# Attention: scores, turned maxima and turned outputs in one ring of three PSUM banks, read by VectorE alone

## The chip, the cores and the metric

The kernel runs on one core of a Trainium2 chip. The metric is the time of one execution in microseconds (us); the median of three runs is given. The engines are TensorE (PE, with its weight loads shown apart as PEld), VectorE (DVE), ScalarE (ACT), GpSimd (POOL) and SyncE (SP), which issues the DMAs.

## The reference

Two layers over x of 4 x 1024 x 128 numbers. Each layer adds an attention and a feed-forward part to x. Both attentions have 16 heads of width 8; the first is causal over 1024 keys, the second has 342 keys, of which a query sees about the first third of its own place:

```
scores = jnp.einsum('bhqd,bhkd->bhqk', q, k)
scores = jnp.where(causal[None, None], scores, -inf)      # layer 1: + mask * -1e9
attn = jax.nn.softmax(scores, axis=-1)
out = jnp.einsum('bhqk,bhkd->bhqd', attn, v)
```

Softmax subtracts each row's maximum, which is the part of it that this change touches.

## The kernel before

The program is a chain of blocks: weights, projection, the first feed-forward part, attention of layer 0, a block between the layers, attention of layer 1, and the experts. `attention` (from L809 on) is one function for both layers.

Its unit of work is a group of four heads of one batch element: 4 batch elements of 4 groups, so 16 units a layer. A unit has two halves that work on the scores in two layouts:

- **fills** (`fill`, L971 to L991 on PE; L1104 to L1111 on DVE): PE writes a block of scores, 128 queries by up to 512 keys (or four heads by 128 keys), with a mask matmul (L984) ahead of the score matmuls (L987), into a PSUM bank. DVE reduces the bank to row maxima (L1111). There are 38 fills in a unit of layer 0 and 17 in one of layer 1. When the last is read, `tail` (L1113 to L1134) splits the maxima into three bf16 parts.
- **turn_max** (L1046, in the prologue L1066): PE turns the parts into a PSUM bank; **copy_max** (L1081) takes them from there to SBUF, and SP stores them as three more rows of the query operand (L891), so that the maxima are subtracted inside the second product.
- **pairs** (L1003) compute the scores once more, transposed, with the maxima in them; ACT takes the exponential (L1089); **weigh** (L1026) multiplies by the values into the bank `a_po`. At the end of 512 queries ACT copies `a_po` to `o_raw` (L1097), **turn_out** (L1055) turns it back with four transposes, and **scale_out** divides by the row sums on DVE (L1146 and L1149).

`batch_schedule` (L725 to L795) writes one list of entries for a batch element by planned PE time, and every engine walks the same list and does its own entries. The fills run ahead of the pairs by one unit and 13 fills. A prologue list (`first`) holds the 38 or 17 fills of the first unit and 13 of the second, with no pairs among them. In layer 0 the batch list stands in a loop for three elements and once more after it; in layer 1 it is written out four times.

PSUM has eight banks: two for fills (`a_ps`), four for the pairs (`a_pst`), one for `a_po`, and one, `p_turn` (`a_pt`), which turn_max and turn_out share. Fill k waits for the reduction of fill k-2 (L977). turn_max and turn_out wait until the former contents of `a_pt` have been read, by ACT (copy_max) or by DVE (scale_out), and the scheduler keeps a copy_max or scale_out ahead of the next turn.

Of the kernel before, what the change touches and what calls it, by code (L numbers as in the profile page):

```python
# [22 lines left out]
ALU = mybir.AluOpType  # L23
# [8 lines left out]
P = 128  # L32
# [12 lines left out]
GH = 4  # L45
# [12 lines left out]
TUNING = [(13, 2800, 300, 2200, 400), (13, 2500, 300, 2200, 200)]  # L58
# [13 lines left out]
        scores_ready maxima_done split_steps maxima_turned maxima_copied maxima_stored scores_t_ready  # L72
        exp_done unseen_zeroed pv_done v_staged o_copied o_turned inverse_done o_done""",
# [602 lines left out]
class Geometry:  # L676
# [3 lines left out]
    def __init__(self, layer):  # L680
# [33 lines left out]

        self.lead, self.tail_time, self.copy_time, self.out_time, self.scale_time = TUNING[layer]

# [8 lines left out]
    def batch_schedule(self, first, last):  # L725
# [5 lines left out]
        if first:  # L731
            return ([("fill", 0, k, 0) for k in range(self.F)] + [("tail", 0, 0, 0)]
                    + [("fill", 1, k, 0) for k in range(2)] + [(what, 0, 0, 0) for what in ("turn_max", "copy_max")]
                    + [("fill", 1, k, 0) for k in range(2, self.lead)])
# [7 lines left out]
        def weigh(step, half):  # L742
# [4 lines left out]
            if half < len(halves):  # L747
                put(4 * (halves[half][1] - halves[half][0] + FIXED), "weigh", g, n, half)
                if st["last"] and half == len(halves) - 1:
                    put(0, "end", g, st["c"], 0)  # L750
                    out.append((now + self.out_time, ("turn_out", g, st["c"], 0)))
                    out.append((now + self.out_time + self.scale_time, ("scale_out", g, st["c"], 0)))
# [17 lines left out]
        for g in range(1, GROUPS if last else GROUPS + 2):  # L770
            for k in range(self.F):
# [5 lines left out]
                if k == self.F - 1:  # L777
                    out.append((at + 1, ("tail", g, 0, 0)))
                    out.append((at + self.tail_time, ("turn_max", g, 0, 0)))
                    out.append((at + self.tail_time + self.copy_time, ("copy_max", g, 0, 0)))  # L780

        ordered, reading = [], None
        for _, entry in sorted(out, key=lambda x: x[0]):
            what, rest = entry[0], entry[1:]
            if what in ("turn_max", "turn_out"):
                if reading:
                    ordered.append(reading)
                reading = ({"turn_max": "copy_max", "turn_out": "scale_out"}[what],) + rest
            if what in ("copy_max", "scale_out"):
                if entry != reading:  # L790
                    continue
                reading = None
            ordered.append(entry)
        return ordered


def counted_before(layer):
# [4 lines left out]
    layer0 = dict(scores_ready=units * geo.F, maxima_done=units * geo.F, split_steps=units * geo.split, maxima_turned=units,  # L802
                  maxima_copied=units, maxima_stored=16 * units, scores_t_ready=2 * units * geo.S,
                  exp_done=2 * units * geo.S, unseen_zeroed=2 * units * len(geo.masked), pv_done=units * geo.S,
                  v_staged=units, o_copied=ends, o_turned=ends, inverse_done=ends, o_done=ends)
# [3 lines left out]
def attention(nc, io, sb, dram, layer):  # L809
# [5 lines left out]
    with ExitStack() as ctx:  # L815
# [24 lines left out]
        block = ctx.enter_context(nc.Block())  # L840

# [34 lines left out]
        def _(sp):  # L876
            def run(b, schedule, last):
                ends = 0
                for what, g, k, part in schedule:
# [8 lines left out]
                    if what == "copy_max":  # L888
                        sp.wait_ge(s["maxima_copied"], since["maxima_copied"] + n + 1)
# [3 lines left out]
                    if what == "next_load" and not last:  # L893
                        sp.wait_ge(s["scores_t_ready"], since["scores_t_ready"] + 2 * S * (n + 1))
                        load_operands(sp, sb, dram, layer, geo.keys, b + 1, g)

# [5 lines left out]
            run(0, geo.batch_schedule(True, False), True)  # L902
# [67 lines left out]
        def _(pe):  # L970
            def fill(b, g, k):  # L971
                f, slot = geo.fills[k], g % GROUPS
                at = (b * GROUPS + g) * F + k
# [17 lines left out]
                last.then_inc(s["scores_ready"], 1)  # L991
# [41 lines left out]
            def run(b, schedule, last):  # L1033
                turned, outs = 1, 0
                for what, g, k, part in schedule:
                    n = b * GROUPS + g
                    if what == "fill":
                        fill(b, g, k)
# [4 lines left out]
                    if what == "turn_max":  # L1043
                        pe.wait_ge(s["split_steps"], since["split_steps"] + geo.split * (n + 1))
                        pe.wait_ge(s["o_done"], since["o_done"] + b * 2 * GROUPS + outs)
                        pe.transpose(p_turn[0:top_rows.shape[0], 0:P // 2].bitcast(BF16),  # L1046
                                     top_parts[:, :, :, :].rearrange("p a j q -> p (a j q)"),
                                     sb["identb"][:, :]).then_inc(s["maxima_turned"], 1)
                        turned += 1
                    if what == "turn_out":  # L1050
                        pe.wait_ge(s["o_copied"], since["o_copied"] + 2 * n + k + 1)
                        pe.wait_ge(s["maxima_copied"], since["maxima_copied"] + b * GROUPS + turned)
                        pe.wait_ge(s["o_done"], since["o_done"] + 2 * n + k)
                        for t in range(CT):
                            last_t = pe.transpose(p_turn[:, t * P:(t + 1) * P], o_raw[:, t * P:(t + 1) * P],  # L1055
                                                  sb["ident"][:, :])
# [928 lines left out]
```

## Time and profile before

| | |
|---|---|
| three runs | 1411.87, 1413.98, 1414.88 us; median 1413.98 us |
| profiled execution | 1409.36 us, span of its profile 1407.4 us |
| PE busy | 1184.2 us, 84% of the span |
| DVE busy | 1041.5 us, 74% |
| ACT busy | 740.0 us, 53% |
| POOL busy | 566.7 us, 40% |
| mean granted TensorE clock | 0.907 of 2.4 GHz |

Attention of layer 0 runs from 246.7 to 793.7 us of the span, that of layer 1 from about 911 to 1160 us. The profile's page gives the busy time of each engine and, in 40 slices, where it lies; other views list the waits of an engine, its instructions in order of time, and sums over stretches that one chooses. A busy PE row has a modelled end, so a wait of PE is looked for in its own idle rows and in the spacing of starts.

### The profile page before, as it was taken

What the parts mean: (1) busy time and instruction counts of PE and PEld (TensorE: products, weight loads), DVE (VectorE), ACT (ScalarE), POOL (GpSimd) and SP (SyncE); (2) the same over time, 40 slices, a digit from 0 to 9 for tenths busy, and PEclk for the clock granted to TensorE, in tenths of its full rate; (3) what the DMA queues carried; (4) which work ended last, traced back from release to release, by engine and by line L of the source; (5) the groups of instructions that cost most, each with busy time, mean ns of one, the idle gap of its engine ahead of it and who ended that gap; (6) DMA issues with size and microseconds to landing.
All of it is one profiled execution on the core that took longest, in us unless ns stands there. A gap on an engine that the chain in (4) does not pass through costs nothing. (4 is left out here: it accounts for less than half of the span.)

```text
span 1407.4 us, 28130 instructions
## 1 busy us (share of the span) xinstructions
PE 1184.2 (84%) x8802; PEld 650.5 (46%) x8802; DVE 1041.5 (74%) x2108; ACT 740.0 (53%) x1137; POOL 566.7 (40%) x821
## 2 busy tenths in 40 slices
PE   0555666899989998999999767589999988999994
PEld 0333555234434443444443344335445436888872
DVE  5997997888868886888785255478778736677788
ACT  0552222056656665666567533136556666777772
POOL 5555222013322331223222155326557663456563
PEclk9987898599999999999999877569999998999996
DMA  3343870001221211121100013112222105577541
GB/s 98 97 124 94 126 92 0 16 4 56 93 81 41 75 62 55 47 69 62 40 2 3 1 57 95 39 35 64 51 61 57 50 23 196 159 237 236 188 120 60
DMA packets 98604, 107.92 MB, mean 77 GB/s; under 512 B 16225, under 2 KB 76454, under 8 KB 98480
## 3 DMA queue, kind: packets, MB, share of 16 engines
q1 hardware_dynamic: 93488, 97.83, 25.5%
q0 software_dynamic: 4992, 8.48, 1.8%
q8 instruction: 73, 1.20, 0.4%
q14 instruction: 51, 0.42, 0.1%
HBM read 64.67 MB, written 42.63 MB: 76 GB/s over the span
## 5 line engine op out<-in xcount | busy, mean ns | idle before, releaser
L1089 ACT ACTIVATE a_probs<-a_pst 128x1024 f32<-128x1024 f32 (+4 forms) x544 | 431.8, 813 | 248.6 <-PE a_pst L1003 245.9
L1111 DVE TENSOR_REDUCE a_tops<-a_ps 128x1 f32<-128x512 f32 (+9 forms) x624 | 363.0, 594 | 93.8 <-PE a_ps L987 78.2
L933 POOL TENSOR_SCALAR_AFFINE_SELECT a_probs<-a_probs 128x256 f32<-128x256 f32 (+3 forms) x384 | 182.3, 481 | 461.8 <-ACT a_probs L1089 460.0
L987 PE MATMUL a_ps<-kp,qp 96*128 96x512 bf16 (+9 forms) x1280 | 329.1, 313 | 8.6 <-issue 6.7
L1003 PE MATMUL a_pst<-qp,kp 99*128 99x512 bf16 (+4 forms) x1088 | 269.1, 335 | 3.2 <-ACT a_probs L1089 2.8
L1026 PE MATMUL a_po<-a_probs,vh 128*32 128x256 f32 (+2 forms) x3584 | 268.9, 373 | 2.5 <-POOL a_probs L933 1.5
L1111 DVE TENSOR_REDUCE a_tops_lead<-a_ps 128x1 f32<-128x512 f32 x256 | 173.0, 690 | 36.3 <-PE a_ps L987 32.8
L987 PEld LDWEIGHTS a_ps<-kp,qp 96*128 96x128 bf16 x1280 | 115.4, 103 | 101.5 <-DVE a_tops_lead L1111 34.8
L984 PE MATMUL a_ps<-mask_s,identb 128*128 128x128 bf16 (+8 forms) x624 | 148.5, 239 | 15.8 <-DVE a_tops L1111 7.1
L984 PEld LDWEIGHTS a_ps<-mask_s,identb 128*128 128x128 bf16 x624 | 60.9, 98 | 167.2 <-DVE a_tops L1111 77.7
L1644 POOL DMA_INDIRECT chosen_rows<-e_slot_y,e_slot_x x92 | 92.7, 1007 | 88.6 <-DVE e_slot_y L1832 66.6
L1003 PEld LDWEIGHTS a_pst<-qp,kp 99*128 99x128 bf16 (+1 forms) x1088 | 97.2, 101 | 67.3 <-ACT a_probs L1089 21.5
L1026 PEld LDWEIGHTS a_po<-a_probs,vh 128*32 128x32 f32 (+1 forms) x3584 | 71.4, 108 | 105.7 <-issue 76.1
L1820 DVE TENSOR_TENSOR e_tails<-e_hidden,e_heads 128x512 fp32r<-128x512 f32 x124 | 91.4, 738 | 35.2 <-ACT e_heads L1754 32.9
L1747 ACT ACTIVATE e_hidden<-e_pup,e_slot_b 128x512 f32<-128x512 f32 x92 | 63.3, 688 | 27.7 <-PE e_pup L1668 25.6
L945 POOL DMA_INDIRECT slot_rows<-rows,slots x64 | 63.2, 988 | 14.2 <-issue 12.2
L1146 DVE RECIPROCAL a_inv_sum<-a_pt 128x16 f32<-128x16 f32 x64 | 16.3, 254 | 63.3 <-PE a_pt L1055 60.8
L148 POOL TENSOR_TENSOR f_hq<-f_v,f_sc 128x704 f32<-128x704 f32 x16 | 22.2, 1385 | 85.2 <-DVE f_v L143 85.2
L594 PE MATMUL f_pt<-ident,f_hq 128*128 128x128 f32 (+1 forms) x96 | 16.1, 310 | 42.9 <-POOL f_hq L148 42.9
L632 ACT ACTIVATE f_hqt<-f_pt 128x256 f32<-128x256 f32 x32 | 12.2, 383 | 66.3 <-PE f_pt L594 66.1
L1097 ACT ACTIVATE a_o_raw<-a_po 128x512 f32<-128x512 f32 x64 | 38.2, 596 | 16.3 <-PE a_po L1026 16.1
L1055 PE MATMUL a_pt<-ident,a_o_raw 128*128 128x128 f32 x256 | 39.5, 276 | 6.5 <-ACT a_o_raw L1097 6.5
(264 smaller groups left out, 1809.4 us busy)
## 6 DMA issues: line engine op xcount, KB each, us to landing
e_slot_w<-weight_parts SPq DMA_DIRECT2D x23, 1024.0 KB, 5.4
weight_parts<-a_cut SPq DMA_DIRECT2D x18, 512.0 KB, 3.9
k_parts<-o SPq DMA_DIRECT2D x48, 128.0 KB
qp<-q_parts SPq DMA_DIRECT2D x64, 96.0 KB
kp<-k_parts SPq DMA_DIRECT2D x32, 192.0 KB
slot_rows<-empty_row SPq DMA_DIRECT2D x4, 1495.0 KB, 27.0
e_slot_x<-slot_rows SPq DMA_DIRECT2D x23, 260.0 KB, 3.5
a_raw<-in_wraw SPq DMA_DIRECT2D x18, 256.0 KB, 4.3
```

The lines of the kernel that those rows point to most:

```text
L933: pool.affine_select(out=seen, in_=seen, compare_op=ALU.is_ge, fill=0.0, base=m0, pattern=[[0, 2], [1, mw]], channel_multiplier=-1 if laye ...
L945: pool.indirect_dma_start(dram["slots"], bass.IndirectOffsetOnAxis(sb["slots"][:, choice, t:t + 1], 0), sb["rows"][:, t, :], None, bounds_ ...
L984: pe.matmul(out, sb["identb"][:, :], mask_s[r][:, 0:mw].unsqueeze(1).broadcast_to([P, nh, mw]), start=True, stop=False, skip_group_check=True)
L987: last = pe.matmul(bank[:, i * room:i * room + w], sb["qp"][slot][0:KROWS, j, f["qt"] * P:(f["qt"] + 1) * P], sb["kp"][slot][0:KROWS, j // ...
L1003: last = pe.matmul(p_st[half][0:st["rows"], i, off:CHUNK], sb["kp"][slot][0:KROWS + PARTS, half, st["kt"] * P:st["kt"] * P + st["rows"]], ...
L1026: last = pe.matmul(p_o[VW * j:VW * (j + 1), c0:c1], sb["vh"][g % 2][0:st["rows"], st["kt"], j, :], probs[local % RING][0:st["rows"], j, c0 ...
L1055: last_t = pe.transpose(p_turn[:, t * P:(t + 1) * P], o_raw[:, t * P:(t + 1) * P], sb["ident"][:, :])
L1089: act.activation(probs[local % RING][0:st["rows"], 2 * part:2 * part + 2, st["off"]:CHUNK], p_st[part][0:st["rows"], :, st["off"]:CHUNK], ...
L1111: dve.tensor_reduce(out, scores, AX.X, ALU.max).then_inc(s["maxima_done"], 1)
L1644: pool.indirect_dma_start(dram["chosen"], bass.IndirectOffsetOnAxis(slot_x[r % XR][:, t, E:E + 1].bitcast(U32), 0), slot_y[r % YR][:, t, : ...
L1747: act.activation(hidden[m % RR][:, :], p_up[m % UR][:, :], ACT.Gelu, bias=biases(j)[:, k:k + 1])\
L1820: dve.tensor_tensor(tails[m % HR][:, :], hidden[m % RR][:, :], heads[m % HR][:, :].bitcast(F32), ALU.subtract)\
```

## The change

`a_pt` and the pair of `a_ps` banks become one ring of three banks. A use of the ring is a fill, a turn_max or a turn_out. Uses are counted in the order of the list; use u goes to bank u mod 3 and waits until the use three before it has been read. One semaphore counts banks filled (by PE), one banks read (by DVE). Because a batch element has 164 uses in layer 0 and 80 in layer 1, both with remainder 2, the first two uses of a batch element find their bank two uses back and the third five back. All reads are now by DVE, in the same order: the copy of the turned maxima leaves ACT (activation Copy) and becomes a DVE `tensor_copy`. `copy_max` and `scale_out` are no longer entries with times of their own; they are done at the place of their turn. The order of PE's own entries stays as it was.

```diff
-TUNING = [(13, 2800, 300, 2200, 400), (13, 2500, 300, 2200, 200)]
+TUNING = [(13, 2800, 2200), (13, 2500, 2200)]
+BANKS = 3
+BANK_USES = ("fill", "turn_max", "turn_out")
...
+    def bank(self, use, first):
+
+        return (use + (self.uses - self.first_uses if first else 0)) % BANKS
...
+    def since_bank(self, use, first):
+
+        if first:
+            return BANKS if use >= BANKS else None
+        return next(d for d in range(1, 2 * BANKS) if (use - d if use >= d else self.uses + use - d) % BANKS == use % BANKS)
...
-        p_s = [ctx.enter_context(nc.psum_tensor(f"a{layer}_ps{i}", [P, 512], F32)) for i in range(2)]
+        p_s = [ctx.enter_context(nc.psum_tensor(f"a{layer}_ps{i}", [P, 512], F32)) for i in range(BANKS)]
...
-        p_turn = ctx.enter_context(nc.psum_tensor(f"a{layer}_pt", [P, 512], F32))
...
+            def fresh_bank(b, use, first):
+
+                behind = geo.since_bank(use, first)
+                if behind:
+                    pe.wait_ge(s["banks_read"], read(b, use - behind, first))
+                return p_s[geo.bank(use, first)]
...
-                if not (isinstance(b, int) and g == 0 and k < 2):
-                    pe.wait_ge(s["maxima_done"], since["maxima_done"] + at - 1)
-                bank, w, nh = p_s[(g * F + k) % 2], f["width"], len(f["heads"])
+                bank, w, nh = fresh_bank(b, use, first), f["width"], len(f["heads"])
...
-                    if what == "turn_out":
-                        pe.wait_ge(s["o_copied"], since["o_copied"] + 2 * n + k + 1)
-                        pe.wait_ge(s["maxima_copied"], since["maxima_copied"] + b * GROUPS + turned)
-                        pe.wait_ge(s["o_done"], since["o_done"] + 2 * n + k)
...
+            def turn_out(b, n, c, use):
+
+                pe.wait_ge(s["o_copied"], since["o_copied"] + 2 * n + c + 1)
+                turned = fresh_bank(b, use, False)
...
-                    if what == "copy_max":
-                        act.wait_ge(s["maxima_turned"], since["maxima_turned"] + n + 1)
-                        act.wait_ge(s["maxima_stored"], since["maxima_stored"] + 16 * n)
-                        act.activation(top_rows[:, :], p_turn[0:top_rows.shape[0], 0:P // 2].bitcast(BF16), ACT.Copy)\
-                            .then_inc(s["maxima_copied"], 1)
...
+            def copy_max(b, n, use, first):
+
+                turned = filled_bank(b, use, first)
+                dve.wait_ge(s["maxima_stored"], since["maxima_stored"] + 16 * n)
+                dve.tensor_copy(top_rows[:, :], turned[0:top_rows.shape[0], 0:P // 2].bitcast(BF16))\
+                    .then_inc(s["banks_read"], 1)
...
+            def scale_out(b, g, c, use):
+
+                turned = filled_bank(b, use, False)[:, :].rearrange("p (t j w) -> p t j w", t=CT, w=VW)
+                dve.wait_ge(s["banks_read"], read(b, use - 1))
```

DVE's order in the prologue of layer 0, around the end of the first unit (`a0_ps0` and so on are the banks, `tops0` and `tops1` the maxima of the two units in flight). Before:

```order
L1133 TENSOR_TENSOR a0_top_parts<-a0_top_rest,a0_top_parts 128x32
L1111 TENSOR_REDUCE a0_tops1<-a0_ps0 128x4
L1111 TENSOR_REDUCE a0_tops1<-a0_ps1 128x2
L1111 TENSOR_REDUCE a0_tops1<-a0_ps0 128x2
L1111 TENSOR_REDUCE a0_tops1<-a0_ps1 128x1
L1111 TENSOR_REDUCE a0_tops1<-a0_ps0 128x1
```

The same place with the change:

```order
L1151 TENSOR_TENSOR a0_top_parts<-a0_top_rest,a0_top_parts 128x32
L1130 TENSOR_REDUCE a0_tops1<-a0_ps0 128x4
L1130 TENSOR_REDUCE a0_tops1<-a0_ps1 128x2
L1158 COPY a0_top_rows<-a0_ps2 96x128
L1130 TENSOR_REDUCE a0_tops1<-a0_ps0 128x2
L1130 TENSOR_REDUCE a0_tops1<-a0_ps1 128x1
L1130 TENSOR_REDUCE a0_tops1<-a0_ps2 128x1
```

The reductions go round three banks, and the copy of the turned maxima (L1158) stands on DVE behind two reductions of the next unit.

DVE's order in layer 1 at the seam between two batch elements, where the last turned output of one element is scaled and the fills of the next begin. Before:

```order
L1146 RECIPROCAL a1_inv_sum<-a1_pt 128x16
L1149 TENSOR_TENSOR o<-a1_pt,a1_inv_sum 128x4x32
L1111 TENSOR_REDUCE a1_tops1<-a1_ps0 128x1
L1111 TENSOR_REDUCE a1_tops1<-a1_ps1 128x1
```

With the change:

```order
L1165 RECIPROCAL a1_inv_sum<-a1_ps1 128x16
L1168 TENSOR_TENSOR o<-a1_ps1,a1_inv_sum 128x4x32
L1130 TENSOR_REDUCE a1_tops1<-a1_ps0 128x1
L1130 TENSOR_REDUCE a1_tops1<-a1_ps1 128x1
L1130 TENSOR_REDUCE a1_tops1<-a1_ps2 128x1
L1130 TENSOR_REDUCE a1_tops1<-a1_ps0 128x1
```

The order of the work is the same; the second fill now uses the bank of the turned output just ahead of it.

## Rows read from the trace of the kernel before

**Rows 1.** Page, part 2: busy tenths in 40 slices of 35.2 us, and granted clock

```profile
PE   0555666899989998999999767589999988999994
PEclk9987898599999999999999877569999998999996
```

**Rows 2.** Busy time by stretch: PE, PEld, DVE, ACT, POOL, clock, DMA share, GB/s

```profile
core 0: us, PE busy (x) PEld busy (x) DVE busy (x) ACT busy (x) POOL busy (x), PEclk, DMA share, GB/s
248.00:283.30 35.30, 30.46 (x93) 7.61 (x94) 31.82 (x56) 1.56 (x2) 0.00 (x0) 0.56 0.06 16
252.30:286.40 34.10, 30.43 (x88) 7.94 (x87) 29.37 (x50) 3.13 (x4) 0.41 (x1) 0.50 0.06 17
300.00:790.00 490.00, 476.85 (x4344) 197.39 (x4336) 373.06 (x673) 310.26 (x417) 137.67 (x296) 0.99 0.16 50
912.70:933.00 20.30, 17.08 (x93) 6.72 (x91) 17.24 (x38) 0.27 (x1) 0.00 (x0) 0.50 0.16 47
993.00:999.70 6.70, 6.48 (x41) 3.26 (x41) 3.37 (x10) 3.93 (x6) 4.22 (x6) 0.50 0.08 22
```

**Rows 3.** Waits of PE, 300 to 790 us: total, times, longest

```profile
PE a_ps L987 <- issue: 6.7, 2, 3.4
PE a_pt L1055 <- ACT a_o_raw L1097: 2.9, 3, 1.0
PE a_pst L1003 <- ACT a_probs L1089: 0.9, 4, 0.3
```

**Rows 4.** Waits of PE, 960 to 1132 us

```profile
PE a_ps L984 <- DVE a_tops L1111: 2.6, 4, 0.8
...
PE a_pt L1046 <- DVE a_top_parts L1133: 2.1, 9, 0.2
PE a_pst L1003 <- ACT a_probs L1089: 0.6, 3, 0.2
```

**Rows 5.** DVE in time, prologue of layer 0: start, length, merged count, idle before

```profile
247.36 6.83 DVE L1111 TENSOR_REDUCE a_tops<-a_ps 128x4 f32<-128x512 f32 x11 [0.96 <-PE a_ps L987]
...
258.02 2.87 DVE L1111 TENSOR_REDUCE a_tops_lead<-a_ps 128x1 f32<-128x512 f32 x4
...
265.99 1.02 DVE L1111 TENSOR_REDUCE a_tops<-a_ps 128x1 f32<-128x384 f32 x2 [0.23 <-PE a_ps L987]
...
274.60 1.28 DVE L1111 TENSOR_REDUCE a_tops<-a_ps 128x4 f32<-128x512 f32 x2
...
282.33 2.07 DVE L1111 TENSOR_REDUCE a_tops_lead<-a_ps 128x1 f32<-128x512 f32 x3
```

**Rows 6.** PE in time, the first pairs after that prologue

```profile
283.47 1.06 PE L1003 MATMUL a_pst<-qp,kp 99*128 99x512 bf16 x2
```

**Rows 7.** Two lines (min/median/max ns) and a row of the page (busy, mean ns)

```profile
L1081 ACT ACTIVATE a_top_rows<-a_pt x32: 263/263/273, 275.1 to 1137.2; 96x128 bf16<-96x128 bf16 x32
...
L1131 DVE CAST a_top_parts<-a_top_rest x32: 181/181/182, 274.3 to 1135.9; 128x32 bf16<-128x32 f32 x32
...
L1146 DVE RECIPROCAL a_inv_sum<-a_pt 128x16 f32<-128x16 f32 x64 | 16.3, 254 | 63.3 <-PE a_pt L1055 60.8
```

**Rows 8.** All engines in time, middle of layer 0

```profile
501.14 1.98 DVE L1111 TENSOR_REDUCE a_tops<-a_ps 128x4 f32<-128x512 f32 x3
...
501.55 0.22 PE L1046 MATMUL a_pt<-identb,a_top_parts 128*96 128x128 bf16 x1
```

**Rows 9.** All engines in time, seam of two batch elements in layer 1

```profile
990.16 0.66 PE L1055 MATMUL a_pt<-ident,a_o_raw 128*128 128x128 f32 x4 [0.71 <-ACT a_o_raw L1097]
...
991.14 0.29 DVE L1149 TENSOR_TENSOR o<-a_pt,a_inv_sum 128x128 f32<-128x128 f32 x1
991.35 1.88 DVE L1111 TENSOR_REDUCE a_tops<-a_ps 128x1 f32<-128x342 f32 x4
...
991.91 0.20 PE L984 MATMUL a_ps<-mask_s,identb 128*128 128x44 bf16 x1 [0.76 <-DVE a_tops L1111]
```

More of the change, by code:

```diff
@@ L732, in batch_schedule @@
             return ([("fill", 0, k, 0) for k in range(self.F)] + [("tail", 0, 0, 0)]
-                    + [("fill", 1, k, 0) for k in range(2)] + [(what, 0, 0, 0) for what in ("turn_max", "copy_max")]
+                    + [("fill", 1, k, 0) for k in range(2)] + [("turn_max", 0, 0, 0)]
                     + [("fill", 1, k, 0) for k in range(2, self.lead)])
@@ L779, in batch_schedule @@
                     out.append((at + self.tail_time, ("turn_max", g, 0, 0)))
[L780 to L794, printed above, removed]
+        return [entry for _, entry in sorted(out, key=lambda x: x[0])]
 def counted_before(layer):
@@ L840, in attention, with filled, read @@
         block = ctx.enter_context(nc.Block())
+        def filled(b, use, first=False):
+            return since["banks_filled"] + geo.uses_before(b, first) + use + 1
+        def read(b, use, first=False):
+            return since["banks_read"] + geo.uses_before(b, first) + use + 1
         def raw_load(sp, b, i):
@@ L876, in _, with run @@
         def _(sp):
-            def run(b, schedule, last):
-                ends = 0
+            def run(b, schedule, last, first=False):
+                ends = use = 0
                 for what, g, k, part in schedule:
@@ L887, in run @@
                         ends += 1
-                    if what == "copy_max":
-                        sp.wait_ge(s["maxima_copied"], since["maxima_copied"] + n + 1)
+                    if what == "turn_max":
+                        sp.wait_ge(s["banks_read"], read(b, use, first))
                         sp.dma_start(sb["qp"][g % GROUPS][KROWS:KROWS + PARTS, :, :].rearrange("r j t -> r (j t)"),
@@ L895, in run @@
                         load_operands(sp, sb, dram, layer, geo.keys, b + 1, g)
+                    use += what in BANK_USES
             if layer == 1:
@@ L990, in fill, with turn_max @@
                                      start=not f["mask"], stop=True, skip_group_check=True)
-                last.then_inc(s["scores_ready"], 1)
+                last.then_inc(s["banks_filled"], 1)
+            def turn_max(b, n, use, first=False):
+                pe.wait_ge(s["split_steps"], since["split_steps"] + geo.split * (n + 1))
+                pe.transpose(fresh_bank(b, use, first)[0:top_rows.shape[0], 0:P // 2].bitcast(BF16),
+                             top_parts[:, :, :, :].rearrange("p a j q -> p (a j q)"),
+                             sb["identb"][:, :]).then_inc(s["banks_filled"], 1)
+            def turn_out(b, n, c, use):
+                pe.wait_ge(s["o_copied"], since["o_copied"] + 2 * n + c + 1)
+                turned = fresh_bank(b, use, False)
+                for t in range(CT):
+                    last = pe.transpose(turned[:, t * P:(t + 1) * P], o_raw[:, t * P:(t + 1) * P], sb["ident"][:, :])
+                last.then_inc(s["banks_filled"], 1)
             def pair(b, g, k, half, local):
@@ L1117, in tail @@
                 top = tops[g % 2]
-                dve.wait_ge(s["maxima_done"], since["maxima_done"] + (n + 1) * F)
+                dve.wait_ge(s["banks_read"], read(b, use - 1, first))
                 if layer == 0:
@@ L1153, in _ @@
-            run(0, geo.batch_schedule(True, False), True)
+                        tail(b, g, use, first)
+                    if what == "turn_max":
+                        copy_max(b, b * GROUPS + g, use, first)
+                    if what == "turn_out":
+                        scale_out(b, g, k, use)
+                    use += what in BANK_USES
+            run(0, geo.batch_schedule(True, False), True, first=True)
             batches(dve, run)
```

94 lines of the change are left out of this document (42 added, 52 removed).

## The prediction

> **What bounds the kernel now.** I read the slices first, then busy time by stretch, then the waits of PE in each stretch, and the timeline only where a wait stood.
>
> The slices show PE at eight or nine tenths through both attentions (slices 8 to 22, and from 28 on). But in the eighth slice the granted clock is down to 5 tenths, and it is at 5 and 6 in the 26th and 27th, where the second attention begins [rows 1]. The stretches say why. In the body of layer 0 (300 to 790 us) PE is busy 476.9 of 490 us at a clock of 0.99, DVE 373 us and ACT 310 us [rows 2]: PE bounds it, and the question is how long PE waits there for what the change touches. It waits 6.7 us at two places with releaser "issue" (the loop's turn), 2.9 us for the copy of `a_po` and 0.9 us for exponentials [rows 3]. No row of PE there waits for a reduction. So in 490 us **the two banks cost PE nothing**.
>
> The two prologues are different. They hold only fills, 51 in layer 0 and 30 in layer 1 (17 and 13), and the clock stands at 0.50, that is 1.2 GHz, from 252.3 to 286.4 us and through 912.7 to 933 us [rows 2]. DVE does the longer job, and still idles: 35.30 - 31.82 = 3.5 us in the first, 20.30 - 17.24 = 3.1 us in the second [rows 2]. Each fill waits for the reduction two before it, and at the low clock it comes too late for DVE. In layer 1 there is a third place: the seam between batch elements, where PE waits 0.76 us for a reduction after 0.71 us for `a_po` [rows 9]; rows 4 give 2.6 us over the three seams.
>
> **The change part by part.** The sum is made against the profiled execution, 1409.36 us, which lies 4.6 us under the median of 1413.98; I apply the difference to the median.
>
> *Third bank, prologue of layer 0.* Two 384-wide reductions that follow without a wait take 1.02 us, so starts are 1.02 - 0.55 = 0.47 apart (one alone is 0.55); two 512-wide ones take 1.28, so 1.28 - 0.69 = 0.60 apart; but four 512-wide ones in the two-bank rhythm take 2.87, or (2.87 - 0.69)/3 = 0.73 apart [rows 5]. Thus a late bank costs more than the idle time, since a waiting reduction also loses its overlap of some 0.08 with the one before. Fifty steps, 12 of them 384 wide, are 12 x 0.47 + 38 x 0.60 = 28.4 us back to back; the trace has the first start at 247.4 and the fifty-first, the second of the last three, at 283.1 us [rows 5]; less some 1.1 us for `tail` that is 34.6 us. The most to be had is 6.2 us, the least the 3.5 us of idle time. PE keeps up: two 512-column matmuls at 1.2 GHz take 1.06 us, 0.43 apart [rows 6], and 512 + 128 columns then some 0.53, under DVE's 0.60. I take **-5.8**, nearer the upper end, because with a third bank a fill may start a whole reduction earlier, and its own 0.5 to 0.6 us fits into that.
>
> *Prologue of layer 1.* Idle 3.1 us as the lower end; a dozen waiting reductions with 0.08 each make 4.0 the upper, but the first four-head fills are many small matmuls, where PE itself is slow. I take **-3.2**.
>
> *The copy of the maxima on DVE.* No row has it. Below it lies DVE's cast of 32 columns, 0.18 us; above it ACT's copy of the same tile, 0.263, and beside it DVE's reciprocal from PSUM, 0.254 [rows 7]. I take 0.25. Once in each prologue it is on the bounding engine: **+0.5** together. The other 30 lie in the bodies, 7.5 us of DVE time under an idle DVE (117 us in layer 0's body), and cost nothing as long as DVE's reductions are not what PE waits for; without that cover they cost 7.5 us. The Trainium skill (Perfetto Trace Analysis, "Optimizing Scalar/DVE Operations") speaks against this move: it gives VectorE a larger fixed access cost to PSUM than ScalarE, about 125 against 51 ns. By its figures the copy would cost 0.07 us more than on ACT, 0.33, and the sum would be 0.2 us less good; no row here compares the two on one tile.
>
> *Order of waits in the body.* DVE now waits for turn_max in its line, with reductions behind it. In layer 0, three reductions start at 501.14 and end at 503.12, while PE's turn is done at 501.77 [rows 8]: DVE reaches the copy at about 502.4, 0.6 us after the turn. PE's next fills come later in PE's own order than the turn, so a waiting DVE would hold up nothing that is ready. A fill with a turn among the three uses before it waits for the same reduction as now; one without waits for an older one. The turn itself waits for a use whose reading lies before `tail` or long ago. Price **0**.
>
> *Seams.* At the seam the turned output takes bank 1, the next fills 0, 1, 2, 0. The second fill, which now goes straight after the first, has to wait for L1149 to end at 991.43, and starts at 991.5. The third finds its bank free, the fourth waits for the first reduction (start 991.35, about 0.5 long) and goes at 991.95, where before the third started at 991.91 and the fourth at 992.33 [rows 9]. **-0.35 each, -1.1** for three. In layer 0 the seam is covered by the 3.4 us of "issue" [rows 3]; SP's store of the maxima follows a copy at nearly the same moment: 0.
>
> *ACT freed of the copy.* 32 x 0.263 = 8.4 us, and it no longer waits in line for the turn. PE waits for ACT's exponentials 0.9 us in layer 0 and 0.6 in layer 1 [rows 3, 4]; I take **-0.3** of it. The 2.1 us for the split maxima [rows 4] stay.
>
> *Clock after the first prologue.* The clock is low until 286.4 [rows 2], 2.9 us after PE's first pairs at 283.5 [rows 6]. If PE gets there 5.5 us earlier, the clock will follow at its own moment; up to twice 2.9 us at half speed would cost 1.5 more. I take **+0.8**.
>
> Sum: -5.8 - 3.2 + 0.5 - 1.1 - 0.3 + 0.8 = **-9.1 us**. The profiled execution becomes 1400.3, the median 1404.9, which I give as 1405.
>
> **The rivals.**
>
> *A: the low clock goes too (1400 to 1402 us).* After two of the seams in layer 1 the clock falls; the first fall is the stretch 993 to 999.7 us at 0.50 with PE busy 6.5 us of it [rows 2], which costs 3.2 us, and it comes right after the two waits of 0.71 and 0.76 us. If shorter waits keep the clock up, some 3 to 5 us come on top: 1400 to 1402. Against it: the first wait stays, and the second is only divided. The Trainium skill (TensorE: Matmul & The Clock Gate, "A second HAM failure mode: psum-queue depth-cycling") describes such swings of the clock from short idle times between banks; by that rule this rival would be the likelier one. 13%.
>
> *B: the third bank buys little (1409 to 1414 us).* If PE at 1.2 GHz is as slow as DVE with masks and weight loads counted, or if a reduction can't start sooner, only the waits over 150 ns go, under 3 us together, and the copies eat 0.5. For it: PE is busy 30.5 of 35.3 us in that prologue [rows 2]. Against: those ends are modelled, and the starts are 0.43 apart when nothing is waited for. A lengthened spell of the low clock after an earlier prologue (1.5 us in each layer) leads to the same place. 22%.
>
> *C: slower, by the seams and the clock (1415 to 1420 us).* The second fill of each batch element now waits for the turned output, in a place where PE has already idled 0.71 us [rows 9]. If that makes the clock fall at all three seams of layer 1 for some 10 us each, 30 us at half speed against the roughly 10 us now, it costs 10 us more; with prologues that give 5 back it is +5. It decides from about 20 us of additional low clock. Against: the idle time of PE at the seam falls by the sum above. 7%.
>
> *D: the bodies' DVE copies hold up fills (1408 to 1412).* Needs DVE late in the bodies, which no wait of PE shows [rows 3]. 3%, counted with B.
>
> **How the numbers follow.** Forecast (1402.5 to 1408.5) 55%, A 13%, B with D 25%, C 7%. About 0.2% (2.8 us) is what a measurement of this kernel can tell from no change. Some two thirds of B lie within it, and a little of it below: faster 0.74, same 0.18, slower 0.08. The range takes in the bounds of both prologues (-6.6 at least, -10.2 at most), most of A and half of B: 1399.5 to 1411.5.
>
> **What would show it.** In the profile after: DVE's 512-wide reductions in the first prologue 0.60 apart, the first pairs at about 277.9 instead of 283.5 us, and layer 1's first pairs a further 3 us earlier against the start of its attention; L1158 at about 0.25 us; PE's waits in 300 to 790 us unchanged; a PE wait of about 0.5 us on L1168 at each seam of layer 1. A copy above 0.4 us, reductions still 0.7 apart, or new PE waits on DVE in the bodies would make it wrong.

## The result, and the profile after

| | before | after |
|---|---|---|
| timed runs | 1413.22 us median of 4 (1411.87 to 1414.88) | 1395.95 us median of 4 (1395.27 to 1397.08) |
| profiled execution, span | 1409.36, 1407.4 us | 1396.07, 1394.1 us |
| mean granted clock | 0.907 | 0.916 |

The ratio is 0.9878, with an interval of 0.9864 to 0.9892: 17.3 us faster, outside the forecast range (1399.5 to 1411.5). The two profiled spans differ by 13.3 us only, as the profiled run of before lies under all its timed runs; the profiled run of after lies among its own. In two later sets of runs the changed kernel stood at 0.9885 [0.9867, 0.9903] and 0.9878 [0.9858, 0.9897]. Line numbers move: fills L984/L987 are now L1001/L1004, the turns L1046 and L1055 are L1013 and L1022, pairs L1035, weighing L1058, exponentials L1105, copy of the raw output L1113, reductions L1130, copy of the maxima L1158, scaling L1168.

Part 2 of the page after, 40 slices of 34.9 us:

```profile
PE   0655666899989998999999767599999978999993
PEclk9877998599999999999999877569999999999997
```

Of the slices at 5 and 6 in [rows 1] those at the two prologues are still there. Busy time by stretch, columns as in [rows 2]: prologue of layer 0, its body, prologue of layer 1, and 7 us from the first seam on.

```profile
248.40:278.60 30.20, 27.30 (x96) 8.61 (x94) 29.84 (x57) 0.42 (x1) 0.00 (x0) 0.60 0.06 19
...
295.00:785.00 490.00, 477.79 (x4348) 197.63 (x4344) 374.14 (x689) 308.03 (x403) 138.25 (x297) 0.99 0.15 50
905.70:921.80 16.10, 14.47 (x93) 7.18 (x92) 15.29 (x37) 0.00 (x0) 0.07 (x1) 0.50 0.20 60
981.00:988.00 7.00, 6.23 (x63) 3.21 (x61) 5.34 (x16) 4.68 (x6) 4.36 (x6) 1.00 0.11 31
```

DVE idles 0.4 us in the first prologue and 0.8 in the second, where it idled 3.5 and 3.1; at the seam the clock is at 1.00, where before it was at 0.50. VectorE in order of time, with the copy's line:

```profile
254.51 2.47 DVE L1130 TENSOR_REDUCE a_tops_lead<-a_ps 128x1 f32<-128x512 f32 x4
...
271.23 1.28 DVE L1130 TENSOR_REDUCE a_tops<-a_ps 128x4 f32<-128x512 f32 x2
272.43 0.21 DVE L1158 COPY a_top_rows<-a_ps 96x128 bf16<-96x128 bf16 x1
272.83 4.94 DVE L1130 TENSOR_REDUCE a_tops<-a_ps 128x2 f32<-128x512 f32 x9 [0.19 <-PE a_ps L1004]
```

```profile
L1158 DVE COPY a_top_rows<-a_ps x32: 205/210/220, 272.4 to 1123.9; 96x128 bf16<-96x128 bf16 x32
```

Four 512-wide reductions take 2.47 us where they took 2.87 [rows 5], so their starts are (2.47 - 0.69)/3 = 0.59 apart. The first pairs, and PE's waits in the body of layer 0, then in 945 to 1117 us of layer 1:

```profile
278.65 0.60 PE L1035 MATMUL a_pst<-qp,kp 99*128 99x512 bf16 x2
```

```profile
PE a_ps L1004 <- issue: 6.3, 2, 3.2
PE a_ps L1022 <- ACT a_o_raw L1113: 2.6, 3, 0.9
PE a_pst L1035 <- ACT a_probs L1105: 0.9, 3, 0.4
```

```profile
PE a_ps L1022 <- ACT a_o_raw L1113: 2.1, 3, 0.7
PE a_ps L1013 <- DVE a_top_parts L1151: 2.1, 9, 0.2
PE a_ps L1001 <- DVE o L1168: 1.5, 3, 0.5
PE a_ps L1013 <- DVE a_tops L1130: 1.5, 3, 0.5
PE a_po L1058 <- ACT a_o_raw L1113: 1.0, 2, 0.5
PE a_pst L1035 <- ACT a_probs L1105: 0.8, 3, 0.3
```

Layer 0's list is that of before [rows 3]. In layer 1 the wait on the scaling (L1168) has come, as said, in the place of the 2.6 us on reductions [rows 4]. The seam in order of time:

```profile
979.37 0.66 PE L1022 MATMUL a_ps<-ident,a_o_raw 128*128 128x128 f32 x4 [0.71 <-ACT a_o_raw L1113]
...
980.35 0.29 DVE L1168 TENSOR_TENSOR o<-a_ps,a_inv_sum 128x128 f32<-128x128 f32 x1
...
980.70 0.19 PE L1001 MATMUL a_ps<-mask_s,identb 128*128 128x44 bf16 x1 [0.51 <-DVE o L1168]
...
981.30 0.59 PE L1035 MATMUL a_pst<-qp,kp 99*128 99x512 bf16 x2
```

From the start of the last weighing matmul to the start of the first pair, which I call the **seam stretch**, it is 3.02 us, against 3.45 before. And the clock, which fell after the seam at 993 us [rows 2], stays up.

### The profile page after: what moved, and what is told of

It reads as the page before. It is cut to its first block and busy times, and to the rows that moved or that the text cites. A ratio compares the mean times of both kernels' runs of the same rounds, so it can differ in the third digit from the quotient of the medians.

```text
span 1394.1 us, 28169 instructions
## 1 busy us (share of the span) xinstructions
PE 1173.7 (84%) x8802; PEld 647.6 (46%) x8802; DVE 1038.0 (74%) x2140; ACT 736.4 (53%) x1105; POOL 568.6 (41%) x821
## 5 line engine op out<-in xcount | busy, mean ns | idle before, releaser
L1105 ACT ACTIVATE a_probs<-a_pst 128x1024 f32<-128x1024 f32 (+4 forms) x544 | 431.9, 813 | 276.1 <-PE a_pst L1035 262.2
L1130 DVE TENSOR_REDUCE a_tops<-a_ps 128x1 f32<-128x512 f32 (+9 forms) x624 | 357.3, 592 | 82.4 <-PE a_ps L1004 69.8
L1004 PE MATMUL a_ps<-kp,qp 96*128 96x512 bf16 (+9 forms) x1280 | 322.7, 312 | 8.3 <-issue 6.3
L1035 PE MATMUL a_pst<-qp,kp 99*128 99x512 bf16 (+4 forms) x1088 | 268.2, 332 | 4.3 <-ACT a_probs L1105 3.2
L1058 PE MATMUL a_po<-a_probs,vh 128*32 128x256 f32 (+2 forms) x3584 | 268.8, 373 | 2.9 <-POOL a_probs L946 1.5
L1130 DVE TENSOR_REDUCE a_tops_lead<-a_ps 128x1 f32<-128x512 f32 x256 | 171.1, 688 | 33.6 <-PE a_ps L1004 31.1
L1004 PEld LDWEIGHTS a_ps<-kp,qp 96*128 96x128 bf16 x1280 | 114.9, 102 | 100.5 <-DVE a_tops_lead L1130 32.0
L1001 PE MATMUL a_ps<-mask_s,identb 128*128 128x128 bf16 (+8 forms) x624 | 148.3, 239 | 9.6 <-PEq L1218 4.5
L1001 PEld LDWEIGHTS a_ps<-mask_s,identb 128*128 128x128 bf16 x624 | 60.6, 98 | 149.7 <-DVE a_tops L1130 55.8
L1035 PEld LDWEIGHTS a_pst<-qp,kp 99*128 99x128 bf16 (+1 forms) x1088 | 96.7, 100 | 70.1 <-ACT a_probs L1105 21.5
L1058 PEld LDWEIGHTS a_po<-a_probs,vh 128*32 128x32 f32 (+1 forms) x3584 | 71.4, 108 | 106.0 <-issue 74.9
L1165 DVE RECIPROCAL a_inv_sum<-a_ps 128x16 f32<-128x16 f32 x64 | 16.5, 257 | 65.8 <-PE a_ps L1022 59.8
L1113 ACT ACTIVATE a_o_raw<-a_po 128x512 f32<-128x512 f32 x64 | 38.3, 599 | 19.6 <-PE a_po L1058 19.5
L1022 PE MATMUL a_ps<-ident,a_o_raw 128*128 128x128 f32 x256 | 39.6, 277 | 6.2 <-ACT a_o_raw L1113 6.2
```

The lines of the kernel that those rows point to most:

```text
L1001: pe.matmul(out, sb["identb"][:, :], mask_s[r][:, 0:mw].unsqueeze(1).broadcast_to([P, nh, mw]), start=True, stop=False, skip_group_check=True)
L1004: last = pe.matmul(bank[:, i * room:i * room + w], sb["qp"][slot][0:KROWS, j, f["qt"] * P:(f["qt"] + 1) * P], sb["kp"][slot][0:KROWS, j // ...
L1035: last = pe.matmul(p_st[half][0:st["rows"], i, off:CHUNK], sb["kp"][slot][0:KROWS + PARTS, half, st["kt"] * P:st["kt"] * P + st["rows"]], ...
L1058: last = pe.matmul(p_o[VW * j:VW * (j + 1), c0:c1], sb["vh"][g % 2][0:st["rows"], st["kt"], j, :], probs[local % RING][0:st["rows"], j, c0 ...
L1105: act.activation(probs[local % RING][0:st["rows"], 2 * part:2 * part + 2, st["off"]:CHUNK], p_st[part][0:st["rows"], :, st["off"]:CHUNK], ...
L1130: dve.tensor_reduce(out, scores, AX.X, ALU.max).then_inc(s["banks_read"], 1)
```

## The experiments

In a kernel's table of stages, "prologue" runs from the first fill to the first pair, "body" from there to the last pair, "between" from layer 0's last pair to layer 1's first fill, "rest" from layer 1's last pair to the end. In brackets: the us of the stage with the clock at 0.50. The last column counts the seams of layer 1 at which the clock fell. One profiled execution each.

| kernel | prologue 0 | body 0 | between | prologue 1 | body 1 | rest | falls |
|---|---|---|---|---|---|---|---|
| before | 36.75 (31) | 506.45 | 122.09 (80) | 20.71 | 221.20 (19.3) | 253.48 | 2 |
| e0 before again | 38.05 (38) | 506.94 | 119.90 (67) | 20.71 | 222.18 (22.1) | 253.65 | 2 |
| after | 31.33 (25) | 506.02 | 120.42 (73) | 16.74 | 218.45 (5.8) | 253.84 | 0 |
| e4 after again | 31.50 (28) | 505.92 | 119.97 (63) | 16.74 | 219.06 (5.8) | 254.01 | 0 |
| e14 after again | 31.33 (25) | 506.33 | 119.78 (66) | 16.75 | 213.79 (2.9) | 253.06 | 0 |
| e1 ring of two | 37.93 (36) | 521.81 | 121.88 (79) | 21.15 | 224.64 (9.4) | 253.19 | 0 |
| e2 three in prologues | 31.51 (28) | 520.00 | 122.53 (79) | 17.17 | 224.53 (9.2) | 253.12 | 0 |
| e3 three in bodies | 38.64 (39) | 505.93 | 120.33 (63) | 20.68 | 216.12 (11.9) | 253.86 | 1 |
| e5 change in layer 0 | 31.33 (25) | 506.18 | 119.76 (66) | 20.74 | 224.45 (19.6) | 253.01 | 3 |
| e6 change in layer 1 | 38.04 (38) | 506.75 | 122.10 (75) | 16.74 | 219.69 (10.5) | | 0 |
| e12 before, short seam | 36.83 (31) | 506.36 | 122.06 (76) | 20.72 | 214.75 (9.0) | 252.86 | 0 |
| e8 copy on ScalarE | 30.81 (21) | 504.45 | 119.94 (66) | 16.75 | 216.64 (9.2) | 252.80 | 1 |
| e7 numbered on | 31.50 (28) | 505.55 | 120.27 (73) | 16.43 | 217.49 (2.7) | 253.17 | 0 |
| e11 numbered on again | 31.33 (25) | 506.30 | 120.09 (69) | 16.43 | 213.44 (3.0) | 253.87 | 0 |
| e10 last turn behind | 31.33 (25) | 506.25 | 120.20 (73) | 16.43 | 210.78 (2.9) | 253.09 | 0 |
| e9 longer seam | 31.33 (25) | 506.11 | 119.96 (73) | 17.49 | 220.50 (19.2) | 254.47 | 1 |
| e13 longest seam | 31.33 (25) | 505.91 | 120.48 (63) | 18.96 | 226.79 (27.2) | 254.03 | 3 |

In the one profiled execution of e6 the last stage took 273.68 us, 19 us more than in any other kernel, with nothing of the change in it; it is left out.

**Parts of the change: e0 to e3.** The four ran on one chip, where before had 1410.4 us (20 runs). e0 is the kernel before unchanged: 1409.6 us, ratio 1.0 [0.9988, 1.0012]. Its profiled execution, 1410.41 us, lies among its timed ones, so the 1409.36 us on which the forecast was built was a quick run of its set.

> The kernel before, unchanged, profiled and timed once more. Theory 1 (the profiled execution of before was a quick one of its kind; the clock falls in other places from run to run): the time is again 1412 to 1415 us, and its profile, if it is a typical one, is some 3 to 5 us longer than 1409.4, with the excess in stretches at the low clock of layer 1 or of the block between the layers, not in the prologue of layer 0. Theory 2 (the two profiles, 13.3 us apart, tell all, and the remaining 4 us of the difference of medians come from something that profiling changes): the profile is again at 1409 to 1410 us.

e1 keeps the one order and VectorE's copy, but has two banks:

```diff
-BANKS = 3
+BANKS = 2
```

> The changed kernel with a ring of two banks; all else as changed (turns in the ring, DVE copies the maxima). Theory 1 (the third bank in the two prologues, and in layer 1's seams, is what pays): the whole gain is gone, 1412 to 1418 us, prologues at 36 to 37 us and 20 to 21 us again. Theory 2 (a good part comes from ACT being freed of the copy and from turns without waits of their own): 1402 to 1408 us. Since turns now also take one of two banks, a loss of some us against before is possible under both.

Measured 1429.69 us, ratio 1.0143 [1.0125, 1.016]. With two banks the shared ring is 19 us worse than two banks and a bank of the turns' own; neither theory had that. Most of it, 15 us, is in layer 0's body, 521.8 against 506.9 us, where PE now waits for reductions:

```profile
PE a_ps L1001 <- DVE a_tops L1130: 4.7, 14, 0.3
...
PE a_ps L1013 <- DVE a_tops L1130: 2.5, 14, 0.3
```

These and 1.2 us more are 8.4 of the 14.9 us; where the others go the list doesn't say.

e2 has three banks, but in the bodies each use waits for the reading two back; e3 is the reverse, two back in the prologues alone:

```diff
-        return next(d for d in range(1, 2 * BANKS) if (use - d if use >= d else self.uses + use - d) % BANKS == use % BANKS)
+        return 2
```

```diff
-            return BANKS if use >= BANKS else None
+            return 2 if use >= 2 else None
```

> Three banks, but in the bodies each use waits for the use two before it; in the prologues for the one three before it. Theory 1: nearly all of the gain stays, 1396 to 1400 us; the prologues as in the changed kernel (31.3 and 16.7 us), the bodies of layer 0 as in both. Theory 3 (the bodies of layer 1 gain from the third bank, by 2 to 4 us, in part by the clock): 1399 to 1402 us, with clock falls after the seams of layer 1.

> The other half: each use of the prologues waits for the use two before it, the bodies as changed. Theory 1: 1409 to 1413 us, prologues 36 to 37 and 20 to 21 us. Theory 3: 1406 to 1409 us. The gains of this run and of the one before it should add up to that of the whole change, 17 us; if they fall short by over 3 us, the clock makes the parts depend on each other.

e2: 1419.44 us, 1.0064 [1.0048, 1.008]; e3: 1405.27 us, 0.9964 [0.9952, 0.9977]. Both lie outside their theories: e2 far above, as the cost of two banks in the bodies was not foreseen, and e3 a little below. Against e1 the third bank is worth 10.3 us in the prologues and 24.4 in the bodies, together 34.7. The changed kernel did not run on this chip; its ratios elsewhere, 0.9878 and 0.9885, would put it at 1393.2 to 1394.2 us here, 35.5 to 36.5 below e1. The parts add up to within 1 to 2 us. Most of the bodies' 24 us only pays back what the shared ring costs with two banks, but not all: e3, with prologues as slow as before, is 5 us faster than before.

**Layer by layer: e4 to e6.** Another chip, before at 1411.95 us. e5 has the changed attention in layer 0 and the old one in layer 1, e6 the reverse.

> The changed kernel, not edited, on the chip of the other runs of this set. Two readings of the first result (1395.95 against 1413.22 us, 17.3 us): the change itself is worth what the two profiled spans differ by, 13.3 us, and the rest was the difference between the profiled run of before and its timed runs; then the ratio here is 0.990 to 0.991 (before near 1410.4, this near 1396 to 1397). Or the whole 17.3 us is the change: 0.988 again. Granted clock: 0.914 to 0.922 as in the first four runs, against 0.897 to 0.911 of before, if the layer 1 part runs at the high clock as a rule; if the one profiled run was luck, some runs show 0.905.

> The changed attention in layer 0 alone, the attention of before in layer 1. By the record's sum for layer 0: -5.8 (prologue) + 0.5 (copy, both layers' half 0.25) + 0.8 (clock after the prologue) and nothing from the bodies: -4.8 us against before, ratio 0.9966. If the bodies of layer 0 gain too from the order of the uses (the theory that the missing 4 us sit there): -9, ratio 0.9936. First pairs near 278.7, last pair of layer 0 near 784.7.

> The attention of before in layer 0, the changed one in layer 1. By the record's sum for layer 1: -3.2 + 0.25 - 1.1 - 0.3: -4.3 us, ratio 0.9970. By the theory that the clock is the missing part (the prologue's columns closer together, so the clock is up earlier, and no fall at the seams): -4.0 prologue, -3 to -5 bodies: -7 to -9, ratio 0.9936 to 0.995, with no stretch at the low clock between 945 and 1150 us. The sum of this and of the run with layer 0 alone should be the whole gain if the two are independent.

e4: 1395.63 us (0.9885), clock 0.914 to 0.921 in all five runs. e5: 1406.38, 0.9956 [0.9925, 0.9987]: -5.6. e6: 1404.19, 0.9939 [0.9923, 0.9956]: -7.8. Together they make 13.3 us of the 16.3 that e4 shows on this chip. The 3 us between lie within the wide interval of e5, so it isn't shown whether the layers depend on each other. Of the microseconds that the forecast missed, layer 1 alone has 3.5 (7.8 for 4.3) and layer 0 alone 0.8 (5.6 for 4.8). In e5 the clock is low at each of the three old seams:

```profile
987.30:990.70 3.40, 3.36 (x21) 1.94 (x21) 2.64 (x9) 1.23 (x2) 0.54 (x1) 0.50 0.09 27
1045.30:1048.70 3.40, 3.40 (x21) 1.87 (x22) 2.70 (x9) 1.09 (x2) 0.40 (x1) 0.50 0.11 31
1103.40:1106.70 3.30, 3.30 (x21) 1.75 (x20) 2.63 (x9) 1.05 (x2) 0.36 (x1) 0.50 0.12 35
```

**The copy's engine: e8.** ScalarE copies the turned maxima again, from the ring's bank:

```diff
-                turned = filled_bank(b, use, first)
-                dve.wait_ge(s["maxima_stored"], since["maxima_stored"] + 16 * n)
-                dve.tensor_copy(top_rows[:, :], turned[0:top_rows.shape[0], 0:P // 2].bitcast(BF16))\
-                    .then_inc(s["banks_read"], 1)
+                dve.wait_ge(s["banks_read"], read(b, use - 1, first))
+                dve.wait_ge(s["maxima_copied"], since["maxima_copied"] + n + 1)
+                dve.sem_inc(s["banks_read"], 1)
```

> The changed kernel, only that the copy of the turned maxima is made by the scalar engine again (from the ring's bank) and the vector engine waits for it in its place before it counts the bank as read. In the prologues nothing stands in the scalar engine's queue: its copy takes 0.26 us against 0.21 and one more handover, +0.1 us each. In the bodies the copy stands behind an exponential of up to 1.0 us and the vector engine, and with it the ring, waits for that: 30 or so times up to 1 us of vector time, hidden if the vector engine's slack in the bodies is real. If the copy's engine matters little (my sum had it at 0.5 us): within 1 us of the changed kernel. If the ring stands still behind it and the tensor engine with it: +3 to +10 us, with waits on the reductions in the list of the bodies.

1393.93 us (1390.05 to 1394.75), 0.9883 [0.9864, 0.9901], the ratio of the changed kernel itself: no cost that shows. Layer 0's prologue is 30.81 us, 0.5 less. The copy's 0.21 us on VectorE is part of that, and the low clock in it is 21 us instead of 25; layer 1's prologue, which has such a copy too, stays at 16.75. In the bodies PE's list has no wait for the copy. The copy's row in this kernel:

```profile
L1096 ACT ACTIVATE a_top_rows<-a_ps x32: 264/268/275, 272.6 to 1120.5; 96x128 bf16<-96x128 bf16 x32
```

**The seam: e7, e9 to e14.** e7 and e11 number the uses of layer 1 on across batch elements, so that a use always waits three back, at the seams too:

```diff
+        if self.layer == 1:
+            return (self.uses_before(b, first) + use) % BANKS
...
+        if self.layer == 1 and not first:
+            return BANKS
```

> The changed kernel with the uses of layer 1 numbered on across the batch elements (always three uses back, no d=2 at a seam). If the 0.5 us that the tensor engine waits at each of three seams for the scaling of the last output is on the path, and gaps of that size are what puts the clock at risk: -1.5 us against the changed kernel, 1394 to 1395, the three waits gone from its list. If those waits lie beside the exponentials' cover: within 0.5 us of the changed kernel, and the wait shows again at the fill or transpose behind it. Slower is not expected.

> The kernel with the uses of layer 1 numbered on once more, beside the other three on one chip: 1393 (1392.4 to 1394.4 before), 2.5 us below the changed kernel's 1395.6 to 1396.0.

e7: 1393.12 us, 2.5 below e4 on its chip; e11 1390.51 on another, where before had 1409.02. The seam stretch stays at 3.02 us, so my 3 x 0.5 us did not go as I said: the wait on the scaling only shrinks to 0.3. It also shortens prologue 1, to 16.43 us. e10 adds to it that the last turned output of a batch element comes behind the third fill of the next:

```diff
+            if b > 0:
+                entries = entries[:at] + [("turn_out", -1, T // CHUNK - 1, 0)] + entries[at:]
```

> Uses of layer 1 numbered on, and the last turned output of a batch element comes behind the third fill of the next one, so that the tensor engine doesn't stand 0.7 us at each seam for the scalar engine's copy of the raw output. Three seams: -0.7 each if the fills there run at once (three free banks), and the scaling's 0.3 us with it: 1390.5 to 1391.5 against 1393.1 of the kernel with the numbering alone. If the vector engine's reductions set the seam's length, as in the prologue: -0.3 each, about 1392.

**1388.44 us, 0.9841 [0.9823, 0.9858]**, 2.1 below e11 on the same chip and the fastest of all. PE in order of time at its first seam, from the last weighing to the first pair (stretch 1.99 us):

```profile
976.64 0.64 PE L1075 MATMUL a_po<-a_probs,vh 86*32 86x256 f32 x8
...
978.25 0.63 PE L1039 MATMUL a_ps<-ident,a_o_raw 128*128 128x128 f32 x4 [0.35 <-DVE a_tops L1147]
...
978.89 0.60 PE L1052 MATMUL a_pst<-qp,kp 99*128 99x512 bf16 x2
```

e9 and e13 lengthen the stretch of the changed kernel: in layer 1's bodies the third use (e9), or the second to fourth (e13), wait for the use just ahead. This is e13's edit:

```diff
+        if self.layer == 1 and not first and 0 < use < 4:
+            return 1
```

> The changed kernel, only that in the bodies of layer 1 the third use (the third fill of a batch element) waits for the read of the second. It lengthens the stretch between the last weighing matmuls of one batch element and the first pair of the next from 3.02 us to 3.4 to 3.7 us, which is what the kernel before has (3.45). If the length of that stretch is what brings the clock down: falls to 0.5 at one to three of the three seams, as in three traces of the kernel before's layer 1 (7 of 9 seams), and +2 to +6 us in all. If it is not: high throughout, and 3 times 0.4 to 0.6, +1.2 to +2 us.

> The changed kernel, only that in the bodies of layer 1 the second, third and fourth use each wait for the read of the use just ahead, so that fill and reduction alternate. The stretch grows from 3.02 us to some 5 us. If its length brings the clock down: a fall at all or nearly all of the three seams (the shorter lengthening had one in three), 5 to 10 us of low clock each, +6 to +12 us against the changed kernel. If the falls are chance that has nothing to do with the length: one fall or none, +5 to +6 us.

e12 shortens that of the kernel before, which keeps its two banks and the bank of its own, by e10's move. In e10 and e12 alike the wait of 0.7 us for the copy of the raw output leaves the stretch, so they change its waits as well as its length.

> The kernel before, with its two banks for scores and its own bank for turned maxima and outputs, only that in layer 1 the last turned output of a batch element and its scaling come behind the third fill of the next element (on the tensor and the vector engine alike). The stretch from the last weighing matmuls to the next first pair shrinks from 3.45 us to about 2.5 us. If a long stretch is what brings the clock down at the seams: no fall at the three seams, and 3 x 0.9 us + the 3 to 4 us that two to three falls cost: -5 to -7 us against before in all. If the falls come from the two banks and not from the stretch: falls as before and -2.5 us.

> The changed kernel beside these two on one chip, as their measure: ratio to before 0.988 to 0.990, high clock at all three seams of layer 1 (one fall in 21 seams of kernels of this form so far).

e9: 1397.15 us, 0.991 [0.9895, 0.9926], stretch 3.73 to 4.00, one fall of 10.2 us; the profiled run, 1400.01 us, was the slowest of its six. e13: 1408.44, 0.9991 [0.9979, 1.0002], stretch 4.93 to 5.20, three falls: 16.7 us above e14 (1391.77, 0.9878) on the same chip, more than I had given. The edit also reaches the first uses of the first batch element, which still lie in the stage of the prologue (18.96 for 16.75 us). Body 1 is 13.0 us longer than in e14; the longer stretches are 6.1 of them, and 6.9 are left for 24 us more at the low clock. Its three low stretches:

```profile
981.10:991.30 10.20, 9.27 (x57) 4.37 (x57) 4.79 (x14) 4.62 (x6) 5.02 (x7) 0.50 0.08 23
1042.50:1052.70 10.20, 9.68 (x59) 4.61 (x60) 4.66 (x13) 4.79 (x6) 5.30 (x9) 0.50 0.05 16
1104.00:1107.40 3.40, 3.34 (x23) 2.02 (x20) 2.27 (x8) 1.94 (x2) 0.84 (x1) 0.50 0.02 5
```

e12: 1403.42, 0.9957 [0.9942, 0.9972], **-5.8 us with the old banks**, stretch 2.06, no fall:

```profile
990.40:1000.00 9.60, 8.30 (x89) 4.29 (x81) 7.19 (x19) 5.85 (x9) 4.93 (x9) 1.00 0.23 52
```

So lengthening the stretch brings falls and shortening it takes them away, and the two banks as such don't bring them. Over all traces: 1.99 to 2.06 us, 0 falls of 6 seams (e10, e12); 3.02 to 3.14, 2 of 24; 3.44 to 3.57 in the old attention, 7 of 9; 3.73 to 4.00, 1 of 3; 4.93 to 5.20, 3 of 3. (The 2 are one each in e3 and e8.) The upper ends of these groups are not causes: where a fall begins inside a stretch it lengthens it, as in e0 (3.57 for 3.44), e8 (3.14 for 3.02) and e9 (4.00 for 3.73). And length is not the whole rule: e1 and e2 have 3.56 to 3.57 with the clock up and no fall in 6, and e9 has fewer falls than the old kernel. What else decides stays open; the counts between 3.0 and 4.0 us are small.

**What a fall costs.** From one seam's first pair to the next, the same kernel in the same trace takes 57.17 us with a fall of 3.4 us in it and 56.33 without (e0), 56.43 and 55.64 (e3), and 59.32 with one of 10.2 us and 56.41 without (e9). So a fall costs some quarter of its length, where rival A had half of it (3.2 us for 6.7). This is an estimate: in the trace of after two such intervals without a fall are 56.73 and 56.13 us.

## Why the prediction was wrong

The direction and the places of the gain were right, the size was half: 9.1 us forecast, 16.3 to 17.5 measured in three sets of runs. One step failed as a mechanism, the clock at the seams of layer 1; the rest of the gap is made of terms of the wrong size and of one stage that the sum did not have. I compare the stages of the kernels with the old code in a stage with those that have the new (means from the table).

- **Prologue of layer 0**, -5.8 and 0.25 for the copy, so -5.55. Against the trace shown it was 36.75 - 31.33 = -5.4: right. But four traces of the old code have 36.75, 38.05, 38.04 and 36.83, the two with the clock low throughout 38.04 and more; the new code has 31.33 to 31.50, since VectorE sets it. The mean gain is 6.0. My one trace happened to be a good one. (In the working, 1.28 - 0.69 is 0.59 and not 0.60, which moves the upper bound of 6.2 us by 0.4.)
- **Prologue of layer 1**, -3.2 + 0.25: measured 20.71 to 20.74 with the old code and 16.74 to 16.75 with the new, -4.0. I took the lower end though the idle time of 3.1 and the lost overlap were both in the rows; no cost of the small matmuls shows.
- **The copy**: 0.21 us for 0.25. By the fixed access costs in the Trainium skill (Perfetto Trace Analysis, "Optimizing Scalar/DVE Operations") it would be dearer than on ScalarE; here it is 0.21 us on VectorE and 0.268 on ScalarE, both from a bank of the ring (e8), and the measurement decides.
- **Order of waits, price 0**: body of layer 0 506.6 (four traces) to 506.1 (after, e4, e5, e14), -0.5: right, but only with three banks. I had not seen what carried that zero: with two, it costs 15 us (e1).
- **Seams**, -0.35 each: the stretch shrank by 0.43. Right, and the wait on L1168 stands where I put it. **The step that failed is the one after it**, that the clock would go on falling there. I gave rival A 13% because "the first wait stays, and the second is only divided"; but with a stretch 0.43 us shorter there are 0 falls in 12 seams (after, e4, e6, e14) for 7 in 9. Body of layer 1: 222.6 us (before, e0, e5) to 217.7 (after, e4, e6, e14; 217.1 without e6), -4.9, for a forecast of -1.1 and -0.3. The low clock in it goes from 20.3 us to 6.3, by 11.3 us at the seams and by 2.8 right behind the prologue. What the seams' falls are worth is an estimate: a quarter of 11.3 us is 2.8; e12 without falls has 214.75 us, with 4.2 us less stretch, and so leaves 3.7 of the mean of the old code, while its timed runs leave 1.6 (5.8 less 4.2). The Trainium skill (TensorE: Matmul & The Clock Gate, "A second HAM failure mode: psum-queue depth-cycling") describes a clock that swings where TensorE idles briefly and often between groups of matmuls, and made rival A the likelier one. The seams of the changed kernel agree with it; e1 doesn't: from 960 to 1110 us PE waits in it 12 times for reductions, 5.6 us in all, where the kernel before has 3 such waits, 2.3 us, and no seam lost its clock.
- **Clock after the prologue**, +0.8: it did not come as said. The clock was up before the first pair at 278.65 us and fell again behind it:

```profile
255.30:275.70 20.40, 19.59 (x66) 6.03 (x66) 20.04 (x40) 0.00 (x0) 0.00 (x0) 0.50 0.04 8
275.80:279.10 3.30, 2.14 (x10) 0.59 (x9) 3.30 (x7) 0.00 (x0) 0.00 (x0) 1.00 0.30 115
279.20:282.50 3.30, 3.30 (x13) 1.49 (x11) 1.77 (x4) 2.50 (x3) 0.82 (x2) 0.50 0.00 0
```

That is 3.4 us low after the first pair for 2.9 before, a quarter of a microsecond at most. The body of layer 0 has as much low clock as before, 17.1 us for 16.6 to 17.8.
- **Between the layers**, a gain that I had nowhere: "between" goes from 121.5 us on average (before, e0, e6, e12) to 120.0 (after, e4, e5, e14), with no line of it changed and less low clock in it. But e0 has 119.9 with the old code, so this one may be chance.
- **Rest**: +0.4.

The means sum to -6.0 - 0.5 - 1.6 - 4.0 - 4.9 + 0.4 = -16.6, against 16.3 to 17.5 measured. Of the 7.5 us between this and the forecast, 3.5 are the clock and body of layer 1, 1.6 "between", 1.5 the two prologues, 1.3 the body of layer 0, where I had charged +0.8 for the clock; the rest stage takes 0.4 back. So the stage of the failed step holds about half of the miss; the falls alone are 1.6 to 3.7 us of it, by the estimates above. Rival A's time (1400 to 1402) was short of it too, as it stood on the same sum. B, C and D are out: DVE idles 0.4 us in the prologue, no seam lost its clock, and layer 0's waits are as before.

## What to carry to other kernels

Giving a ring more kinds of use can cost more than the bank that it frees is worth: here two banks with the turns among the fills cost 19 us, and the third bank gave some 35 back. So try the shared order and the number of banks apart. Where a granted clock falls at a short stretch of waiting matmuls, price the fall with the stretch (here 0.4 us less of it took part in a gain of 4.9 us over three seams, and 1.4 us less gave 5.8), by what a fall costs in the trace and not by half of its length, and look for work that can go between, as the fills in front of the last turned output did. And take a stage's length from more than one trace before taking a small difference from it: the prologue of one and the same kernel was 36.75 and 38.05 us.

## What the runs showed that was not expected

- The prologue of layer 0 hardly feels TensorE's clock any more: 31.33 us with 25 us of low clock and 31.50 with 28, where before it had 36.8 us with 31 and 38.0 with 38. VectorE is busy 20.04 of 20.40 us at the low clock and 3.30 of 3.30 at the high one (rows in the part before): with the third bank its pace sets the prologue, and PE's hardly does.
- One kernel, two paces: body 1 of the changed kernel takes 218.45 us in one trace and 213.79 in another (e14), both with the clock up at the seams. The first has two waits of 0.5 us of the weighing matmuls for the copy of the raw output (L1058 on L1113), the second none. They are worth 1 us. Another 2.2 us lie between the first pair and the first seam, where the first trace has one more low stretch (5.8 us for 2.9); where the rest goes was not settled. This spread, 4.7 us, is as large as the gain of 4.9 us in the means of body 1, so the seams' share rests on the falls counted and the intervals compared within one trace, more than on those means.
